# Gated delta attention on one core: values convolved by VectorE, and the head of the next chunk's inverse moved into the present step

## The reference

```python
mixed = x @ qkv_w.T                      # then a causal convolution over time, 4 taps, per channel
q, k, v = split(conv(mixed));  z = x @ z_w.T
beta = sigmoid(x @ b_w.T);  alpha = exp(-exp(A_log) * softplus(x @ a_w.T + dt_bias))
# token by token
S = S * alpha;  S = S + outer(k, (v - k @ S) * beta);  o = q @ S
o = o * rsqrt(mean(o * o) + eps) * norm_w * (z * sigmoid(z))
out = o @ out_w.T                        # summed over the heads, added to the residual stream
```

## Time and profile before

| | us |
|---|---|
| median of three runs (8049.25, 8056.37, 8074.13) | 8056.37 |
| profiled execution, its own time | 8045.66 |
| its span | 8043.8 |
| PE / DVE / ACT / POOL busy over the span | 6799.7 / 5751.5 / 3577.8 / 2800.7 |
| the 67 steps, first weights' turn to the last addition into X | 1024 to 2583 |

### The profile page before, as it was taken

The page is one execution under the profiler, slowest core; times in us unless marked ns, Lnnn a source line. Parts: engine busy times, 40 slices in busy tenths (PEclk is TensorE's granted clock), DMA queues, the critical chain, the costliest instruction groups (busy, mean ns, idle before and its releaser), DMA issues. The chain is left out here.

```text
span 8043.8 us, 271416 instructions
## 1 busy us (share of the span) xinstructions
PE 6799.7 (85%) x118712; PEld 4816.6 (60%) x118712; DVE 5751.5 (72%) x10171; ACT 3577.8 (44%) x6436; POOL 2800.7 (35%) x1921
## 2 busy tenths in 40 slices
PE   7999789999998898898998998998997798445566
PEld 3444478888886566666665665665664555345434
DVE  6666379999997786786885885885886577842366
ACT  3555245555554565564664664664664222210121
POOL 0110023332332673673773773773772000011000
PEclk8999599999999999999999999999998899555557
DMA  0000000000000321221221221221220000000000
GB/s 15 1 1 1 2 6 5 4 4 4 4 3 10 78 73 48 69 75 44 73 74 43 73 75 42 76 75 42 76 76 17 16 1 2 2 3 4 5 0 14
DMA packets 187953, 249.14 MB, mean 31 GB/s; under 512 B 58998, under 2 KB 85493, under 8 KB 185845
## 3 DMA queue, kind: packets, MB, share of 16 engines
q1 hardware_dynamic: 186740, 231.40, 11.0%
HBM read 27.84 MB, written 2.10 MB: 4 GB/s over the span
## 5 line engine op out<-in xcount | busy, mean ns | idle before, releaser
L1702 POOL TENSOR_TENSOR XNT<-XNT 128x1024 f32<-128x1024 f32 x384 | 907.0, 2362 | 317.9 <-DVE XNT L1871 312.8
L1773 PE MATMUL wa_front<-w_wqkv,wa_xT 128*128 128x512 f32 x1920 | 941.4, 614 | 30.0 <-ACT wa_qT L1766 11.1
L1705 POOL TENSOR_TENSOR XNT<-XNT,wa_rnorm 128x1024 f32<-128x1024 f32 x320 | 608.7, 1902 | 256.6 <-ACT wa_rnorm L1728 232.2
L1773 PEld LDWEIGHTS wa_front<-w_wqkv,wa_xT 128*128 128x128 f32 x1920 | 334.7, 194 | 296.6 <-issue 256.7
L1868 DVE TENSOR_TENSOR XNT<-wa_front,w_scaled 128x1024 f32<-128x1024 f32 x320 | 390.3, 1220 | 159.4 <-PE wa_front L1773 159.4
L447 PE MATMUL a0h_ring<-a0h_QT,a0h_KT 32*128 32x512 f32 (+3 forms) x1536 | 443.8, 549 | 14.4 <-ACT a0h_E L565 10.4
L565 ACT ACTIVATE a0h_E<-a0h_ring 128x512 f32<-128x512 f32 (+1 forms) x640 | 320.5, 555 | 279.9 <-PE a0h_ring L447 278.6
L1871 DVE TENSOR_TENSOR XNT<-wa_front,w_scaled 128x512 f32<-128x512 f32 x640 | 409.2, 681 | 0.0
L1878 DVE TENSOR_REDUCE wa_least<-wa_sq 128x16 f32<-128x1024 f32 x320 | 380.0, 1187 | 14.6 <-ACT wa_sq L1720 12.6
L1720 ACT ACTIVATE wa_sq<-wa_front 128x1024 f32<-128x1024 f32 x320 | 326.0, 1020 | 133.4 <-PE wa_front L1773 105.2
L1779 PEld LDWEIGHTS wa_front<-consts,XNT 128*128 128x128 f32 x2560 | 277.9, 142 | 158.4 <-POOL XNT L1705 109.5
(11 more groups left out here) (621 smaller groups left out, 17523.9 us busy)
## 6 DMA issues: line engine op xcount, KB each, us to landing
wa_v_look<-wa_v_all SPq DMA_DIRECT2D x960, 128.0 KB, 2.4
wa_v_look<-wa_v_all SPq DMA_DIRECT2D x640, 64.0 KB, 2.1
wal_v_look<-wal_v_all SPq DMA_DIRECT2D x192, 128.0 KB, 2.4
wal_v_look<-wal_v_all SPq DMA_DIRECT2D x128, 64.0 KB, 2.1
w_wqkv<-in_L_ffn_Wqkv_dram SPq DMA_DIRECT2D x6, 1024.0 KB, 6.4
w_wo<-in_L_ffn_Wo_dram SPq DMA_DIRECT2D x6, 512.0 KB, 6.9
w_wqkv<-in_L_ffn_Wqkv_dram SPq DMA_DIRECT2D x12, 256.0 KB, 7.7
f2w_raw<-in_L_ffn_w_dram SPq DMA_DIRECT2D x48, 64.0 KB, 1.9
```

The source lines that it names most:

```text
L1702: g.tensor_tensor(rot[:, at], rot[:, at], part[:, at], ALU.add).then_inc(s[summed], 1)
L1705: g.tensor_tensor(rot[:, at], rot[:, at], spread(rnorm[:, at, :], HDW), ALU.mult).then_inc(s[done], 1)
L1773: last = pe.matmul(front[:, first + i, :], x_of(which), wqkv[:, (2 * n + i) * 512:(2 * n + i + 1) * 512], start=True, stop=True)
```

## The change

It edits `delta_chunk_steps` and its buffers only. Values are produced raw by one 512-wide product like keys and queries, kept in a third row of `hist`, convolved by VectorE into `vconv` and turned by TensorE. The four scaled weights, `xs` and its copies go. Gram, N, Nc, lev, XTc and T now belong to chunk j at the end of step j, so that `zt(1)` opens the next step. The sum of log decays is one 512-wide product of `ga` (now g x upto) with `after`. `place` goes to GpSimd as one masked product. The scaling by rstd moves from y to the addition into X. The lists of all four engines are reordered.

The other lists, cut to their core:

```diff
 ScalarE
-    Nc(q), yT(e), keys' turn(q), keep_raw(0), evict_z(1), keep_raw(1), evict_z(2), squares, evict_z(3), sqrt,
-    evict_z(4), E(j), values(q), T64a, evict_z(5), T64b, tanh(q), evict_z(6)
+    evict_z(1), yT(e), E(j), evict_z(2), keys' turn(q), keep_raw(0), evict_z(3), evict_z(4), keep_raw(1), T64a,
+    keep_raw(2), evict_z(5), T64b, values(q), evict_z(6), Nc(j), squares(r), tanh(q), sqrt(r)
 GpSimd
-    xs(j), newS(r), lev0(q), lev(q), sb(j), Estrict(j), Eincl(j), history
+    newS(r), sb(j), Estrict(j), Eincl(j), x4(q), lev(j), history
```

```diff
 VectorE
+                ga(j)                                    # upto x g
                 if r is not None:
                     kS, R
-                ga(j), XTc(q), T(q), X += out(e), u(r), uend(r), o(r) = qS x decay
+                grow(1)
+                AT(q), o(r) = qS x decay
+                grow(2)
                 convolve(0, 0, 1)
+                u(r)
+                grow(3)
+                uend(r)
+                convolve(0, 1, T0)
+                grow(4)
+                    for b in range(G):
+                        last = v.scalar_tensor_tensor(out=mine[:, b], in0=bank[2][:, b, :], scalar=rstd[:, b:b + 1],
+                                                      in1=mine[:, b], op0=ALU.mult, op1=ALU.add)
                 o += AT u (r)
+                convolve(1, 0, 1)
+                x5 copies, S(r), N(j)
+                convolve(1, 1, T0)
+                x6 copy, y(r) = o x gatez
                     v.wait_ge(s["tanh_ready"], q + 1)
                     gatez(q)
+                convolve(VC, 0, 0)
+                if j is not None:
+                    v.wait_ge(s["lev_ready"], j + 1)
+                    v.tensor_tensor(XTc[:], lev[:, 0], ident, ALU.add).then_inc(s["X_ready"], 1)
+                    v.transpose(flat(T[:]), flat(XTc[:])).then_inc(s["T_ready"], 1)
+                convolve(VC, 0, T0, False)
                 if r is not None:
-                    chain(v.reciprocal(rstd[:], std[:]))
-                    v.tensor_tensor(y[:], y[:], spread(rstd[:], P), ALU.mult).then_inc(s["y_ready"], 1)
+                    v.reciprocal(rstd[:], std[:]).then_inc(s["rstd_ready"], 1)
```

```diff
-                    four_of(bank[7], lambda b: ga[:, b, :], lambda b: c.upto, s["dt_ps"])
+                    pe.matmul(flat(bank[2][:]), c.after, flat(ga[:]), start=True, stop=True).then_inc(s["dt_ps"], 1)
-                    for n in range(TAPS):
-                        last = pe.matmul(bank[3][:, b, :], xs[:, q % 2, b, n:n + P], weights(q)[:, V_W + n, :], start=(n == 0),
-                                         stop=(n == TAPS - 1))
+                    pe.matmul(flat(bank[0][:]), weights(j)[:, V_W, :], x_of(j), start=True, stop=True).then_inc(s["raw_ps"], 1)
+                    turn_four(bank[3], vconv[:, q % 2], s["vtok_ps"])
```

More of the change, by code:

```diff
@@ L1085, in tx @@
                         pe.wait_ge(s["x4_ready"], q + 1)
+                        if e is not None:
+                            pe.wait_ge(s["added"], e + 1)
+                        elif j is not None:
+                            pe.wait_ge(s["E_ready"], j + 1)
                         hi = quarter(1)
@@ L1212, in keep_weights @@
                     a.wait_ge(s["loaded"], 8 * 16 * (n + 1))
-                    if n >= 1:
-                        a.wait_ge(s["w_ps"], 2 * n)
-                    for i in reversed(range(TAPS)):
-                        last = a.activation(raw_w[:, 2 if i == 0 else 4 + i, :], raw_w[:, 2, :], ACT.Copy,
-                                            scale=taps[:, n % 2, 2, i:i + 1])
-                    last.then_inc(s["scaled"], 1)
                 a.wait_ge(s["w_ps"], 2 * n + 1 + part)
@@ L1250, in keep_raw @@
                     a.activation(hist[:, n, :, T0:], bank[at][:], ACT.Copy).then_inc(s["raw_copied"], 1)
-                if q is not None:
-                    a.wait_ge(s["N_ready"], q + 1)
-                    if q >= 1:
-                        a.wait_ge(s["lev_ready"], q)
-                    for n in range(4):
-                        last = a.activation(Nc[quarter(n)], N[quarter(n), :, quarter(n)], ACT.Copy)
-                    last.then_inc(s["Nc_ready"], 1)
+                evict_z(1)
                 if e is not None:
@@ L1363, in _, with convolve @@
                     decay = [spread(of_chunk(decays[:, n], r), P) for n in range(2)]
[L1365 removed]
+                def convolve(n, first, end, begin=True):
                     if j is None:
                         return
[L1368 to L1371 removed]
+                    into = vconv[:, j % 2] if n == VC else conv[:, j % 3, n]
+                    t = taps[:, j // BLOCKS % 2, 2 if n == VC else 1 - n]
+                    if first == 0 and begin:
+                        v.wait_ge(s["raw_copied"], 3 * j + n + 1)
                         chain(v.tensor_scalar(into, hist[:, n, :, T0:], t[:, T0:TAPS], None, ALU.mult))
@@ L1388, in grow @@
                     v.transpose(flat(T[:]), flat(XTc[:])).then_inc(s["T_ready"], 1)
-                def place():
-                    for k in range(4):
-                        last = v.tensor_copy(XT[quarter(k), slot, :, quarter(k)], XTc[quarter(k)])
-                    last.then_inc(s["x4_ready"], 1)
-                if q is not None:
-                    v.wait_ge(s["gram_ps"], q + 1)
-                    v.wait_ge(s["strict_ready"], q + 1)
-                    v.tensor_tensor(N[:], bank[0][:], Estrict[:], ALU.mult).then_inc(s["N_ready"], 1)
+                if j is not None:
+                    if j >= 1:
+                        v.wait_ge(s["dt_ps"], j)
+                    v.tensor_tensor(ga[:], c.upto.unsqueeze(1).broadcast_to(four),
+                                    spread(of_chunk(g_all[:], j), P),
+                                    ALU.mult).then_inc(s["ga_ready"], 1)
                 if r is not None:
@@ L1436, in _ @@
                     v.tensor_tensor(o[:], bank[5][:], o[:], ALU.add).then_inc(s["o_done"], 1)
+                convolve(1, 0, 1)
+                if q is not None:
+                    v.wait_ge(s["x_ps"], LX * q + 5)
+                    for lo, hi in BLOCK_PAIRS:
+                        last = v.tensor_copy(XT[quarter(lo), slot, :, quarter(hi)], bank[4][quarter(lo), :, 0:32])
+                    last.then_inc(s["x5_ready"], 1)
+                if r is not None:
                     if r % BLOCKS < BLOCKS - 1:
```

311 lines of the change are left out of this document (148 added, 163 removed).

## The result

The changed kernel takes 8212.15 us (median of 4 runs, 8207.20 to 8217.97) against 8063.31 for the kernel before in the same session: 1.0186 times as long, with an interval of 1.0166 to 1.0205. It is slower by 149 us. The forecast was 8150 with a range of 7975 to 8225. The profiled execution took 8214.47 us, its span 8212.5.

What follows compares the result with a forecast made beforehand. TensorE's list set the old step, VectorE close behind; after the change both sum to about 20.4 and 20.5 us but wait for each other. (25.4 + 0.1 - 23.96) x 62 = +95 us gives 8150, range 7975 to 8225.

Steps and rivals of the forecast that it cites:

- The walk (steps 1 to 7): One new step followed through the engines' lists from VectorE's ga as time 0; it closes at 25.4 us.
- Step 6, y: VectorE reaches y at 19.6 while GpSimd's lev runs; y ends at 21.37, gatez runs 21.29 to 21.98.
- y ahead of lev: -0.2: Bound on the step if VectorE's y runs before GpSimd's lev instead of behind it: -0.2 us.
- y twice its length: Sign in the next profile that the forecast is right: VectorE's y takes twice its length beside GpSimd's lev.
- The clock: Rival: TensorE idles 19.2 to 22.0, its clock falls in half the steps; +1 us per step, 8212; 7 in 100.
- The table load: ScalarE's load ahead of exp: a switch costs 1.3 us; hidden ahead of its wait or not, 0 either way.
- the engines overlap: Rival: TensorE and VectorE hide behind each other; 21.8 us per step, 7922 (7890 to 8010); 17 in 100.
- Only the end is shorter: Rival: squares or lev no longer hold gatez back; step 24.3, +22 us, 8078 (8025 to 8100); 13 in 100.
- The placement as cause: TensorE idles 5 us per step, VectorE 4, because of where work stands in ScalarE's and VectorE's lists.
- the two rows named: Nc, squares, tanh in one ScalarE row before gatez; three taps and the reciprocal ahead of ga on VectorE.

Runs made afterwards that it cites:

- e4: Changed kernel plus two 512-wide TensorE products per step behind level 6's last product, results unread; 8150.40 us, 1.0115 of the kernel before.
- e8: Changed kernel with tanh ahead of squares, ga and grow(1) earlier, level 2 evicted ahead of exp, two unread filler products; 8112.82 us, 1.0055 of kernel before.
- e9: e8 with only the keys' first tap ahead of u, the other three behind uend; 8021.67 us, 0.9944 of the kernel before.
- e1: Changed kernel with tanh ahead of the four squares on ScalarE, no fillers; 8165.14 us, 1.0133 of the kernel before.
- e6: Kernel before in its old order with only the values' part: raw product, turn, four VectorE taps; 8239.64 us, 1.0209 of the kernel before.
- e11: e10 without its two filler products; 8100.90 us, 1.0041 of the kernel before.
- e10: e9 with the values' first tap moved behind XTc and T; 8068.20 us, 0.9989 of the kernel before.
- e12: e9 with one unread filler product per step instead of two; 8026.89 us, 0.9942 of the kernel before.

## Why the prediction was right or wrong

**The walk (steps 1 to 7) was right to 0.3 us, at full clock.** e4, the changed lists at clock 1.00, lets it be laid beside the trace, from ga as 0: raw keys end at 6.2 (walk 6.25), their copy runs from 6.3 to 6.9 (6.29 to 6.89), zt(4) starts at 9.5 (9.47), N at 16.9 (16.95), tanh ends at 21.1 (21.1). The step closes at 25.07 instead of 25.4. The waits are the listed ones: 2.81 us ahead of k·S, 1.33 for raw keys' copy, tanh right behind the squares. TensorE's busy time without the fillers is (1078.91 / 1200) x 25.07 - 1.98 = 20.6 us, against 20.4 added up. VectorE's is (983.07 / 1200) x 25.07 = 20.5, as stated, although the terms that the forecast lists for it (18.5 - 0.61 - 0.9 + 2.7 + 0.46) give only 20.2.

**Step 6, y, was wrong.** It was to end 0.54 behind lev, at 21.37, on the model of y x rstd behind newS in the earlier trace rows. But there VectorE started second; here it was at work (the x6 copy, 0.05 ahead of lev) and y followed at once. y kept its 0.68 and lev took the 0.84. gatez then waited for tanh alone and started at 21.1 instead of 21.29, which is 0.2 of the 0.3 between 25.4 and 25.07. The bound "y ahead of lev: -0.2" covered it; the signs "y twice its length" and the model behind it did not hold.

**The clock was the term that was left out of the sum.** The forecast of 8150 has it at nothing, and set it apart as a rival of 7 in 100, worth +1 us a step and 8212 in all, "if half of the steps lose it". The measured price is 0.95 us a step (e4). Nearly all steps lose it, 62 of 63, and what they lose is in part hidden: in the step shown k·S, zt(1) and q·k take 1.5 us longer, but raw keys start 5.58 us behind ga instead of 5.24 (e4). So the price was right, the chance was not, and the condition was not what happened. The walk itself put a 2.8 us idle piece into every step, and the earlier trace rows showed what 3.9 us had done; that it was one of the forecast's own consequences should have put it into the sum.

That the measured median is the rival's 8212 to the microsecond is luck. The rival stands for +157 us in the steps (25.5 + 1.0 - 23.96, 62 times) on 8056. Measured were +129 us in the steps and 20 us outside them, which nobody foresaw, on 8063. The own range, 8100 to 8200, was left by 12 us; the outer range, 7975 to 8225, held the result because it had been drawn to take in most of the rival.

**The table load** costs what its row said. exp's load starts at 1735.79, while the decays' product that exp waits for still runs (to 1735.99), and exp follows it at 1737.09: 1.3 us and no more, part of it under the wait. The Trainium skill's drain of 1.38 us (ScalarE: Activation LUTs, What ACT_TABLE_LOAD costs) is not in these rows either.

**The rival "the engines overlap"** (21.8 us) needed gatez not to hang on the row of ScalarE and the step's head not on ga. Both moves together (e8) reach 24.3, so these two conditions were not enough; a third, which the forecast did not have, is that the keys' second tap, which meets GpSimd, does not stand ahead of u. With it e9 takes 22.78 on the mean, 1.1 less than the kernel before and 1.0 more than this rival. **"Only the end is shorter"** (24.3) was refuted for the change, as tanh stayed behind the squares; e1's move at full clock gives 24.7.

**The placement as cause** was half right. By mean steps the clock is worth 0.95 us (the change to e4), the two rows named 0.56 at full clock (e4 to e8), and the keys' second tap ahead of u, with its meeting with GpSimd, 1.64 (e8 to e9); together 3.15, from 25.93 to 22.78. The change is faster than the kernel before only with all three dealt with: e8, which leaves the third, is slower, and so is e6 in the old order.

## What to carry to other kernels

When work is moved so that an engine idles in one piece of some 3 us in each step, put the half-clock length of what stands behind it into the sum at once, and try a product that nobody reads in the gap. In e6 the clock fell behind short waits close together, so read the granted clock and not the longest wait alone. When work is moved onto VectorE, lay its list against GpSimd's: an instruction that later work waits for should not stand behind one that can start just after a GpSimd instruction. Price each move at full clock: tanh's was worth 0.3 us a step there and 0.84 beside the falling clock. And look after each edit whether two instructions have changed places in time: without its fillers e11 is another kernel than e10 in ga as well.

## What the hardware showed that was not expected

- An idle piece of 2.81 us was enough: the next 3.40 us ran at a granted clock of 0.54, where 0.74 us in each step (e12) left it at 1.00 and 1.80 us (e11) gave 0.93 over the middle of the stage. Two products of 0.9 us that nobody reads bought back 60 us. In e6, with a clock of 0.84, it fell behind four pieces of 0.20 to 0.92 us within 6 us.
- 0.12 us in the start of ga against Estrict (0.05 ahead, 0.07 behind) made ga 1.10 us longer and Estrict 0.46 shorter.
- A TENSOR_SCALAR with a single tensor input suffers from GpSimd as well: 1.17 us beside lev, 1.49 beside Eincl, 0.48 alone.
- lev, which began 0.05 us behind a VectorE copy, was held through the y that followed it too (2.37 instead of 1.53); whether by the copy's claim or by y's own was not tried.
